# A two-layer attention and FFN kernel: the attention output, turned and normed by way of DRAM instead of by TensorE transposes

## The reference, cut to what matters

```python
x = L0_attn_x                                   # (2, 512, 512)
for l in (0, 1):
    xn = layernorm(x)
    x = x + attention_l(xn) + ffn_l(xn)         # layer 0's FFN begins with an RMS norm
# attention: q, k, v of 32 heads (layer 0: 8 groups of k, v), causal softmax(q k^T / 4) v
#   ctx = (softmax(scores) @ v).transpose(0, 2, 1, 3).reshape(b, t, 512);  out = ctx @ Wo + bo
# ffn: (silu(n @ gate) * (n @ up)) @ down, of inner width 1792 (layer 0) and 1376 (layer 1)
```

## Time and profile before

| | |
|---|---|
| median of 3 runs | 898.31 us |
| profiled execution | 898.58 us |
| its span | 896.4 us |
| PE, DVE, ACT, POOL busy | 848.9, 537.4, 451.4, 404.2 us |
| instructions | 16589 |
| mean granted TensorE clock | 0.989 of full speed |
| DMA | 96.32 MB, 107 GB/s |

### The profile page before, as it was taken

How to read it: one execution, slowest core, us unless ns; L and a number is a source line. 1 busy time by engine, 2 the same in 40 slices (tenths; PEclk the granted TensorE clock), 3 DMA queues, 4 the chain that set the end, 5 groups by cost and what they waited for, 6 DMA issues and landing times.

```text
span 896.4 us, 16589 instructions
## 1 busy us (share of the span) xinstructions
PE 848.9 (95%) x5803; PEld 648.2 (72%) x5804; DVE 537.4 (60%) x1584; ACT 451.4 (50%) x812; POOL 404.2 (45%) x551
## 2 busy tenths in 40 slices
PE   8889999999889999999999999999999999999987
PEld 5866666567578766677778887677677797766777
DVE  8646557767648575745667567655567465555433
ACT  3333445556537364444565555444466455445633
POOL 3233434445444444444435464344454655444543
PEclk9999999999999999999999999999999999999999
DMA  6672242541542525237282643727356553822220
GB/s 203 165 164 69 77 80 82 116 105 58 139 94 59 104 60 141 75 122 134 73 154 74 160 104 99 155 66 157 82 141 122 138 150 99 165 69 63 69 79 29
DMA packets 52882, 96.32 MB, mean 107 GB/s; under 512 B 7992, under 2 KB 11064, under 8 KB 52792
## 3 DMA queue, kind: packets, MB, share of 16 engines
q1 hardware_dynamic: 52800, 95.26, 43.5%
HBM read 78.92 MB, written 16.25 MB: 106 GB/s over the span
## 4 chain that ended last, share of the span: by engine, by line
PE 85%; DVE 9%; issue 2%; ACT 2%; POOL 1%; DMA 0%; POOLq 0%; SPq 0%; ACTq 0%; DVEq 0%
PE g_ring L1270 40%; PE acc L1270 24%; PE s_bank L1393 7%; PE g_ring L1433 6%; PE t_bank L1413 4%; DVE s_bank L1234 3%; PE g_ring L1443 1%; DVE h_lo L1213 1%; PE g_ring L1316 1%; DVE xt_lo L1151 1%; DVE qk_parts L1173 1%; DVE xt_lo L1161 1%; DVE gate L1198 0%; ACT qk_parts L1063 0%; DVE maxima L1234 0%
## 5 line engine op out<-in xcount | busy, mean ns | idle before, releaser
L979 POOL TENSOR_TENSOR w_lo<-w_raw,w_hi 128x512 fp32r<-128x512 f32 x204 | 265.0, 1301 | 188.7 <-ACT w_hi L1021 185.5
L1234 DVE CUSTOM_DVE_ANT_0 s_bank<-s_bank,causal 128x128 f32<-128x128 f32 (+3 forms) x512 | 236.6, 518 | 42.2 <-PE s_bank L1393 41.7
L1001 POOL TENSOR_SCALAR_AFFINE_SELECT p<-p 128x256 f32<-128x256 f32 (+1 forms) x320 | 117.7, 369 | 287.3 <-ACT p L1014 280.3
L1270 PE MATMUL g_ring<-xt_hi,w_hi 128*128 128x512 f32 (+1 forms) x504 | 211.7, 420 | 10.9 <-DVE xt_lo L1164 5.0
L1270 PE MATMUL g_ring<-xt_lo,w_hi 128*128 128x512 f32 (+1 forms) x504 | 200.8, 398 | 0.0
L1270 PE MATMUL g_ring<-xt_hi,w_lo 128*128 128x512 f32 (+1 forms) x504 | 200.1, 397 | 0.0
L1021 ACT ACTIVATE w_hi<-w_raw 128x512 fp32r<-128x512 f32 x204 | 127.7, 629 | 132.0 <-PE g_ring L1270 74.2
L1014 ACT ACTIVATE p<-t_bank 128x512 f32<-128x512 f32 x320 | 173.7, 595 | 38.2 <-PE t_bank L1413 32.2
L1270 PEld LDWEIGHTS g_ring<-xt_hi,w_hi 128*128 128x128 f32 (+1 forms) x504 | 96.1, 191 | 48.8 <-issue 12.2
L1270 PE MATMUL acc<-w_hi,h_hi 128*128 128x256 f32 (+1 forms) x400 | 118.0, 295 | 4.7 <-DVE h_lo L1213 4.7
L1213 DVE TENSOR_TENSOR h_lo<-h,h_hi 128x512 fp32r<-128x512 f32 (+1 forms) x100 | 86.9, 879 | 46.2 <-ACT h_hi L1070 45.9
(11 more groups left out here) (90 smaller groups left out, 1078.9 us busy)
## 6 DMA issues: line engine op xcount, KB each, us to landing
w_raw<-weights_in SPq DMA_DIRECT2D x204, 256.0 KB, 2.7
qk_scratch<-qk_parts SPq DMA_DIRECT2D x24, 512.0 KB, 3.0
q_op<-qk_scratch SPq DMA_DIRECT2D x96, 128.0 KB, 5.0
k_op<-qk_scratch SPq DMA_DIRECT2D x48, 128.0 KB, 6.5
k_op<-k_scratch SPq DMA_DIRECT2D x48, 64.0 KB, 2.8
x<-x_in SPq DMA_DIRECT2D x8, 256.0 KB, 3.7
y_out<-x SPq DMA_DIRECT2D x8, 256.0 KB, 2.2
k_scratch<-qk_parts SPq DMA_DIRECT2D x2, 512.0 KB, 3.6
```

Of the source, the lines that this page charges most:

```text
L979: pool.tensor_tensor(w_lo[:, c % SPLIT, :], w_raw[:, c % RAW, :], w_hi[:, c % SPLIT, :].bitcast(F32), ALU.subtract).then_inc(split_done, 1)
L1001: pool.affine_select(out=view, in_=view, compare_op=ALU.is_ge, fill=0.0, base=0, pattern=[[0, n], [1, P]] if n == 2 else [[1, P]], channel ...
L1234: last = dve.tensor_tensor_reduce(out=bank[:, at:at + n], in0=bank[:, at:at + n], in1=causal[:, 512 - n:], scale=1.0, scalar=LOWEST, op0=A ...
L1270: ins = pe.matmul(dst, w[a], xa[c], start=first and i == 0, stop=last and i == 2, skip_group_check=skip)
```

## The change

The steps otr and ctr go, with the array recip. After oev, SP writes o_t of each quad to a DRAM scratch ("oout"). Behind the second quad of an octet, "oin" reads twice: the 8 x 16 rows of output into one tile of `context`, now [128 features, 4, 512 tokens], and the 8 rows of sums, each spread over 16 partitions, into o_t. "norm" runs once an octet: a reciprocal of o_t over 128x512, in place, and a multiplication of the tile of context by it. chi and clo read context in SBUF. The planner no longer has the ctr steps in the fill list and no otr queue; an o tile waits for the clo of its own octet, and HEADS of the first phase is 4 instead of 12. oev of a quad waits for the write of the octet's first quad, or for the norm of the last octet, since o_t is one buffer that serves for both.

```diff
-PE_US = {"xtr": 0.44, "ctr": 0.44, "proj": 2.73, "v0": 5.4, "v1": 2.83, "out": 1.42, "ST": 0.75,
-         "Mt": 0.17, "PV": 2.6, "otr": 0.44}
+PE_US = {"xtr": 0.44, "proj": 2.73, "v0": 5.4, "v1": 2.83, "out": 1.42, "ST": 0.75,
+         "Mt": 0.17, "PV": 2.4}
...
-          "norm": 1.35, "hlo": 0.7}
+          "norm": 1.3, "hlo": 0.7}
...
-         "store": 0.43, "bo1": 0.43, "oout": 0.4, "oin": 0.8}
+         "store": 0.43, "bo1": 0.43, "oout": 0.4, "oin": 1.0}
...
+O_WRITE, O_READ = 5.0, 10.0
...
-HEADS = (12, 0, 0, 7)
-CTX_AT = 3
+HEADS = (4, 0, 0, 7)
...
     def ctx_tile(ph, slot, kt):
-        g = take("g")
-        e = pe_step(max(after("norm"), after("g", g - 2)), "ctr", g, kt)
-        if kt == KT - 1:
-            end["ctr", ph] = e
-        hi = place("act", max(e, after("x_read", slot)), "chi", g, slot, kt)
-        end["g", g] = end["x", slot] = place("dve", hi, "clo", g, slot, kt)
+        hi = place("act", max(end["norm", KT * ph + kt], after("proj_read", slot)), "chi", ph, slot, kt)
+        end["clo", KT * ph + kt] = place("dve", hi, "clo", ph, slot, kt)
...
-    def out_ready(l, slot, kind, tile, i, first):
+    def out_ready(l, b, slot, kind, tile, i, first):
+        octet = KT * PHASES.index((l, b)) + tile
+        if kind == "o" and at("norm", KT * PHASES.index((l, b)) + KT - 1) == NEVER:
+            return NEVER
+        if kind == "o" and at("clo", octet) == NEVER:
+            hi = gap("act", max(end["norm", octet], after("proj_read", slot)), ACT_US["chi"]) + ACT_US["chi"] + SIGNAL["act"]
+            return max(hi + DVE_US["clo"] + SIGNAL["dve"], freed("acc", state["acc"], 2) if first else 0.0)
         r = max(freed("acc", state["acc"], 2), freed("acc", state["acc"] + 1, 2)) if first else 0.0
-        r = max(r, at("x", slot) if kind == "o" else after("h"))
+        r = max(r, at("clo", octet) if kind == "o" else after("h"))
...
+        if kind == "o" and nh == 0 and tile == 0:
+            for kt in range(KT):
+                ctx_tile(PHASES.index((l, b)), slot, kt)
         if i == 0:
             state["w"] = chunk(("o" if kind == "o" else "d", l, nh, tile // 2))
         w = state["w"]
-        ready = max(ready, end["split", w], at("x", slot) if kind == "o" else 0.0)
+        ready = max(ready, end["split", w],
+                    end["clo", KT * PHASES.index((l, b)) + tile] if kind == "o" else 0.0)
...
-        end["g", g] = end["oev", u] = place("act", max(e, after("otr", u - 1)), "oev", g, u)
-
-    def otr_ready(u):
-        first = after("ctr", u // QUADS - 1) if u % QUADS == 0 and u >= QUADS else 0.0
-        if u % QUADS == 0 and u >= QUADS and at("ctr", u // QUADS - 1) == NEVER:
-            return NEVER
-        return max(at("oev", u), after("g", state["g"] - 2), first)
-
-    def otr(u):
-        g = take("g")
-        e = end["otr", u] = pe_step(max(at("oev", u), after("g", g - 2)), "otr", g, u)
-        end["g", g] = end["norm"] = end["norm", u] = place("dve", e, "norm", u, g)
-
+        end["g", g] = end["oev", u] = place("act", max(e, after("oout", u - 1) if u % 2 else after("norm", u // 2 - 1)),
+                                                      "oev", g, u)
+        octet = u // 2
+        end["oout", u] = place("sp", max(end["oev", u], after("norm", octet - 2)), "oout", u) + O_WRITE
+        if u % 2:
+            free = max(end["oout", u], after("norm", octet - 1), after("clo", octet - KT))
+            here = place("sp", free, "oin", octet) + O_READ
+            end["norm", octet] = place("dve", here, "norm", octet)
...
-            if nh == 0:
-                at_tile = min(HEADS[ph] + CTX_AT, FT[l])
-                w[at_tile:at_tile] = w_ctx(ph, slot)
...
-    queues = {"visit": [], "Mt": [], "O": [], "pinned": pinned}
+    queues = {"visit": [], "Mt": [], "pinned": pinned}
...
-        queues["O"].append((where(u + 1, OTR_AT), lambda u=u: otr_ready(u), lambda u=u: otr(u)))
...
-        context = sb("context", [P, TT, D], F32)
+        context = sb("context", [P, KT, T], F32)
...
+                elif kind == "oout":
+                    u = s[1]
+                    octet = u // 2
+                    sp.wait_ge(oev_done, n_oev[u])
+                    if octet >= 2:
+                        sp.wait_ge(o_here, 32 * (octet - 1))
+                    sp.dma_start(o_scratch[octet % 2, u % 2 * P:u % 2 * P + P, :], o_t[:, :]
+                                 ).then_inc(o_out[u % 2], 16)
+                elif kind == "oin":
+                    octet = s[1]
+                    for i in range(2):
+                        sp.wait_ge(o_out[i], 16 * (octet + 1))
+                    if octet >= KT:
+                        sp.wait_ge(clo_done, n_clo[(octet // KT - 1, octet % KT)])
+                    if octet:
+                        sp.wait_ge(norm_done, n_norm[octet - 1])
+                    heads = o_scratch[octet % 2].rearrange("(j r) t -> j r t", j=8)
+                    sp.dma_start(context[:, octet % KT, :], heads[:, 0:HD, :]).then_inc(o_here, 16)
+                    sp.dma_start(o_t[:, :], heads[:, HD:VW, :].to_broadcast([8, HD, T])).then_inc(o_here, 16)
...
                     act.wait_ge(pv_done, 4 * n_pv[u])
-                    if u:
-                        act.wait_ge(work_done, n_otr[u - 1])
+                    if u % 2:
+                        act.wait_ge(o_out[0], 16 * (u // 2 + 1))
+                    elif u:
+                        act.wait_ge(norm_done, n_norm[u // 2 - 1])
...
+                elif kind == "chi":
+                    _, ph, slot, kt = s
+                    act.wait_ge(norm_done, n_norm[KT * ph + kt])
+                    act.wait_ge(work_done, ctx_after[ph])
+                    act.activation(xt_hi[:, slot, kt, :], context[:, kt, :], ACT.Copy).then_inc(chi_done, 1)
...
+                elif kind == "clo":
+                    _, ph, slot, kt = s
+                    dve.wait_ge(chi_done, n_chi[(ph, kt)])
+                    dve.tensor_tensor(xt_lo[:, slot, kt, :], context[:, kt, :],
+                                      xt_hi[:, slot, kt, :].bitcast(F32), ALU.subtract).then_inc(clo_done, 1)
...
-                    _, u, g = s
-                    dve.wait_ge(work_done, n_otr[u])
-                    if u % QUADS == 0 and u:
-                        dve.wait_ge(work_done, ctx_used[u // QUADS - 1])
-                    sums = g_ring[g % 2][:, :].rearrange("p (q j c) -> p q j c", q=TT, j=4)
-                    link(dve.reciprocal(recip[:, :, :], sums[:, :, :, HD]))
-                    c0 = (u % QUADS) * 4 * HD
-                    dve.tensor_tensor(
-                        context[:, :, c0:c0 + 4 * HD].rearrange("p q (j d) -> p q j d", j=4),
-                        sums[:, :, :, 0:HD], recip[:, :, :].unsqueeze(3).to_broadcast([P, TT, 4, HD]),
-                        ALU.mult).then_inc(g_freed, 1)
+                    octet = s[1]
+                    dve.wait_ge(o_here, 32 * (octet + 1))
+                    link(dve.reciprocal(o_t[:, :], o_t[:, :]))
+                    dve.tensor_tensor(context[:, octet % KT, :], context[:, octet % KT, :], o_t[:, :], ALU.mult
+                                      ).then_inc(norm_done, 1)
...
-                elif kind == "ctr":
-                    _, g, kt = s
-                    wait_g(g)
-                    phase = ctrs.index(s) // KT
-                    pe.wait_ge(g_freed, n_norm[QUADS * phase + QUADS - 1])
-                    for tt in range(TT):
-                        last = pe.transpose(g_ring[g % 2][:, tt * P:(tt + 1) * P],
-                                            context[:, tt, kt * P:(kt + 1) * P], ident[:, :])
...
+                    if kind == "v1":
                         pe.wait_ge(g_freed, x_free_count[s])
+                    elif s in o_steps:
+                        pe.wait_ge(clo_done, n_clo[(o_steps[s], s[4])])
...
-                elif kind == "otr":
-                    _, g, u = s
-                    wait_g(g)
-                    pe.wait_ge(oev_done, n_oev[u])
-                    for tt in range(TT):
-                        last = pe.transpose(g_ring[g % 2][:, tt * P:(tt + 1) * P],
-                                            o_t[:, tt * P:(tt + 1) * P], ident[:, :])
...
+    o_scratch = nc.dram_tensor("o_scratch", (2, 2 * P, T), F32).ap()
```

102 lines of the change are left out of this document (44 added, 58 removed).

## The result

| | before | after |
|---|---|---|
| median (lowest to highest) | 898.4 us (896.46 to 899.17, 4 runs) | 937.35 us (928.05 to 942.12, 4 runs) |
| ratio after / before | | 1.0406, 95% interval 1.0372 to 1.044 |
| profiled execution, its span | 898.58, 896.4 us | 942.12, 939.9 us |
| PE busy / PE idle in the span | 848.9 / 47.5 us | 856.7 / 83.2 us |
| mean granted TensorE clock | 0.989 | 0.947 |

The forecast was 889 us, in 870 to 907. The sign was wrong, and the size by 48 us.

A forecast was written before the change was run, and what follows sets the result against it. PE's instruction stream was taken as the bound. From 898.6 us: -18.9 for transposes, -5 idle time, +2.7 tail, +12 for stalls behind slow norms, giving 889.4, stated as 889 us, range 870 to 907.

The forecast's parts named there:

- The reciprocal's own time: On DVE, one 128x512 reciprocal per octet: 3.4 us, from the line through the reciprocal's two smaller measured rows.
- B: Rival: the reciprocal on DVE is fast, no stalls, shorter tail chain; 874.5 us, range 870 to 880, chance 0.28.
- The stall per norm: PE waiting behind DVE's late norm: 0.8 us for each of 15 norms, 12 us, bounds 0 to 28.
- C: Rival: slow norm falls where PE has no slack, from 1.4 us a norm; 899 to 916 us, chance 0.22.
- A: Main case: slow reciprocal, PE's gain larger than DVE's stalls; 889 us, own range 880 to 897, chance 0.42.
- The transposes' slots: On PE, 43 groups of four transposes (otr, ctr) outside the tail removed, 0.44 us each: 18.9 us gained.
- 5 us of idle time more: PE's idle time ahead of the removed transposes and around otr, taken as 5 us won, bounds 0 and 10.
- rival D: Planned DMA times make the order wait at phase ends and for late loads, eating the gain; near 898, chance 0.08.
- The way through DRAM: 64 added DMAs, 16 MB, on SP's queue: taken as 0, riding in SP's idle time.
- ACT's new wait: On ACT, oev waits for the first quad's write or the last norm: cost taken as 0.
- The tail: Behind the last PV, a chain of 14.3 us to the last octet's output against 11.6 before: 2.7 us lost.
- the note on a dip: The longer tail wait may buy one stretch at half clock, some 1.7 us, not in the middle sum.

The follow-up runs named there:

- a_norecip: The changed kernel with each 128x512 reciprocal of o_t replaced by a multiplication by 0.5, same order, waits and DMAs; 899.19 us, ratio 1.0029.
- b_recip: The kernel before with 16 reciprocals of a 128x512 SBUF tile added on DVE, one at every second quad's norm; 950.93 us, ratio 1.0619.
- n_tuned: a_norecip with planner settings moved (EARLY 6, HEADS 2, 0, 0, 0, last visits 3 us apart); leaves the division out; 884.95 us, ratio 0.9851.
- a_small: The changed kernel with sums read as 128x32, inverted, written to a DRAM scratch and read back spread, plan told; 915.0 us, ratio 1.0204.
- a_tail: a_small with the last phase's HEADS 7 to 0 and the last visits due 3 us apart, not 10; 902.76 us, ratio 1.004.
- best1: a_small with sums read ahead of context under their own semaphore, shorter landings in the plan and other settings moved; 916.24 us, ratio 1.0222.
- a_split: The changed kernel with each reciprocal cut into four of 128x128, each a planned step of its own; 926.77 us, ratio 1.0324.
- a_late: a_tail with planned landings of sums and reciprocals later (7.0 and 6.0 us), EARLY and HEADS moved; 893.95 us, ratio 0.9962.

## Why the prediction was wrong, step by step

**The reciprocal's own time: right.** 3.35 us measured, 3.4 forecast from the line through the two small rows. The same line, 149 + 6.3 n ns, gives 0.35 at n = 32 and 0.95 at n = 128; 0.35 and 0.953 were measured. So B was out from the start. The Trainium skill's iterative divide with a repeat count of 8 ("VectorE: DVE Perf Modes", First, the fixed hardware budget), read as eight cycles an element, gives the estimated 4.3 us, which is above the 3.35 us measured.

**The stall per norm: the term that failed.** It was taken as 0.8 us for 15 norms, 12 us. The pair after and a_norecip gives 38.2 us, or 2.4 for each of 16. Its two halves, from the profiled executions: idle 22.5 us, 1.4 a norm, inside the bounds of 0 and 1.9 but at C's point of decision. The mark that was to tell A from C, PE's waits on gate, h, maxima and h_lo, went from 16.4 to 35.2 us, 19 more, which lies between A's 15 and C's 21 and decides nothing; all of PE's waits on DVE went from 35.7 to 65.3. The other half is 21.0 us of busy time, 1.3 a norm, for which the sum had no term. The half clock was priced once, at 1.7 us, for the tail and outside the sum. It comes behind waits in the middle too: 100 us at 1.2 GHz against 45. (In the other executions of the changed kernel, whose clock is higher, the second half is smaller.) The choice of 0.8, "a bit below the middle", leaned on DVE's idle 40%. b_recip shows that this idle time is no cover: the work of DVE beside its plan is paid in full, because PE waits for what DVE gives next in its order, the maxima and the banks of g_ring.

**The transposes' slots: right as work, wrong as time.** 43 x 0.44 = 18.9 us, and 21.5 us of busy time less in n_tuned, tail included. But the sum took them, and 5 us of idle time more, straight off the end, "nothing hides this gain". In the order of the changed kernel it all came back: a_norecip has 13.2 us less busy and 13.2 more idle than before. That is the size of rival D (near 898; 899.19 measured), which got 0.08. Of D's two marks the first is missing: ahead of the tail PE waits once for a split of context in the changed kernel, 2.7 us, and not more than 3. The second shows: waits for q_op and its m rows and for k_op are 5.1 us there and 6.2 in a_norecip, and none before. So D's name for the loss, the order, holds: moved, it gives 14 us (n_tuned), with 1.9 us of these waits left. (There a wait of 3.3 us for a split of context does stand, at 254.9.) And even in that order idle time grew by 3.6 us instead of falling by 5. The mark "PE busy down by 26 to 29 us" missed as well, by the overlap that the prediction itself takes off the busy time of the rows: 21.5 at equal clock.

**The way through DRAM: taken as 0, and not quite free.** The waits for q_op and k_op just named are the ones that the prediction listed for a cover that is gone. ACT's new wait, taken as 0 too, is 13.2 us in four times for the norm ahead of an oev in the changed kernel. Not seen was that DVE can stand before a landing: 15.7 to 36.1 us a kind in a_small, a_tail and best1.

**The tail: right in its chain, with some luck in the sum.** 14.7 us against 14.3; the single wait of 8.7 us lies in the 6 to 9 named. The last read took 5.5 us, not 4.0, and the other links together 1.2 us less than forecast (the write 2.1 to the next issue, not 2.6). The prediction's five handovers of 0.1 also stand in its sum as 0.6. With the half clock behind it the stretch from PV's start to the end grew from 896.4 - 853.12 = 43.3 us to 49.7, 6.4 more, where the sum had 2.7 and the note on a dip 1.7.

**Sum by the runs.** 898.4, + 0.8 for the change in its order without reciprocals (-21.2 forecast for slots, idle time and tail), + 38.2 for the reciprocals (+12 forecast): 937.4. The mechanism was C, at 0.22, with D's loss on top. C's upper end was 915.5 because each rival was given only one of the two losses, C's stall ended at 1.9 a norm where 2.4 were measured, and the clock had one dip in the tail and none in the middle.

**What stays open.** Why the better order is better: three or four settings were moved at once. How a_split's 11 us divide, and how a_late's 8.8. Which new wait on SP or ACT holds the loads and exponentials that PE waits for in a_norecip. Another engine for the reciprocal was not tried.
